# A four-layer graph kernel: the preparation ahead of its first stage reordered, part of it placed in that stage's first turn

## The reference

```python
# layer 0: two graph convolutions, then an LSTM over windows of length p = 1..4
h = relu(einsum('ts,bsh->bth', adj, x @ Wg0 + bg0))
h = relu(einsum('ts,bsh->bth', adj, h @ Wg1 + bg1))
for p in range(1, MAX_SKIP + 1):
    nw = Tv // p
    wins = h[:, :nw * p, :].reshape(Bv * nw, p, Hd)
    last = _lstm_last(Wih[p - 1], Whh[p - 1], bih[p - 1], bhh[p - 1], wins)
    h = h.at[:, arange(nw) * p + (p - 1), :].set(last.reshape(Bv, nw, Hd))
# layer 1: causal attention, scores + adj as mask; uses Wq Wk^T and Wv Wo
# layer 2: diagonal, upper and lower parts of adj with three weights W[k]
# layer 3: attention over 256 edges (src, dst), segments by src
e = einsum('behd,hd->beh', leaky_relu(Xq[:, src] + Xq[:, dst], 0.2), a)
e = e + log(adj[src, dst] + 1e-8)
attn = segment_softmax(e, src);  Y = segment_sum(attn * Xv[:, dst], src)
```

## Time and profile before

| | us |
|---|---|
| median of three runs | 1332.06 (1331.55 to 1334.45) |
| the profiled execution's own time | 1332.07 |
| its span, first to last instruction | 1330.3 |
| PE busy | 1208.8 (91%) |
| DVE busy | 1020.4 (77%) |
| ACT busy | 834.2 (63%) |
| POOL busy | 345.8 (26%) |
| mean granted TensorE clock | 0.977 of full speed |

### The profile page before, as it was taken

How to read it: one execution, slowest core, us unless ns; L and a number is a source line. 1 busy time by engine, 2 the same in 40 slices (tenths; PEclk the granted TensorE clock), 3 DMA queues, 4 the chain that set the end, 5 groups by cost and what they waited for, 6 DMA issues and landing times. The chain is left out here.

```text
span 1330.3 us, 25504 instructions
## 1 busy us (share of the span) xinstructions
PE 1208.8 (91%) x7808; PEld 1028.3 (77%) x7808; DVE 1020.4 (77%) x2892; ACT 834.2 (63%) x1836; POOL 345.8 (26%) x587
## 2 busy tenths in 40 slices
PE   2899999999899999999989799997999899978998
PEld 1678788787787877878878678876777688856998
DVE  6677877878778777787787699997777578776776
ACT  3476575675757757757567577775777376752332
POOL 3110200201002001020020122224667488842332
PEclk7899999999999999999999999998999899988999
DMA  9300000000000000000000000000000000001222
GB/s 272 84 1 1 1 1 1 0 0 0 0 0 0 0 0 0 0 0 0 0 1 1 1 1 0 0 0 1 1 0 0 0 2 1 2 1 32 75 75 71
DMA packets 24707, 20.85 MB, mean 16 GB/s; under 512 B 1744, under 2 KB 20304, under 8 KB 24400
## 3 DMA queue, kind: packets, MB, share of 16 engines
q1 hardware_dynamic: 24656, 20.21, 5.3%
HBM read 11.82 MB, written 8.39 MB: 15 GB/s over the span
## 5 line engine op out<-in xcount | busy, mean ns | idle before, releaser
L565 ACT ACTIVATE gate<-ps,b_lstm 128x256 f32<-128x256 f32 (+2 forms) x624 | 300.2, 557 | 36.8 <-PE ps L592 36.8
L590 PE MATMUL ps<-H_hi,w_hi 128*128 128x256 f32 (+2 forms) x624 | 212.7, 342 | 42.1 <-ACT gate L565 25.2
L591 PE MATMUL ps<-H_hi,w_lo 128*128 128x256 f32 (+2 forms) x624 | 205.4, 330 | 0.0
L592 PE MATMUL ps<-H_lo,w_hi 128*128 128x256 f32 (+2 forms) x624 | 196.1, 335 | 6.6 <-DVE H_lo L534 5.3
L575 ACT ACTIVATE tanh_c<-cell 128x512 f32<-128x512 f32 (+2 forms) x176 | 90.4, 514 | 127.7 <-DVE cell L525 81.7
L590 PEld LDWEIGHTS ps<-H_hi,w_hi 128*128 128x128 f32 x624 | 117.6, 189 | 68.1 <-ACT gate L565 32.6
L134 POOL TENSOR_SCALAR rstd<-mv 128x8 f32<-128x8 f32 x18 | 12.5, 694 | 601.0 <-DVE mv L107 600.9
L592 PEld LDWEIGHTS ps<-H_lo,w_hi 128*128 128x128 f32 x624 | 114.8, 189 | 25.1 <-DVE H_lo L534 17.4
L591 PEld LDWEIGHTS ps<-H_hi,w_lo 128*128 128x128 f32 x624 | 118.0, 189 | 7.7
L590 PE MATMUL ps<-hid_hi,w_hi 128*128 128x256 f32 (+2 forms) x384 | 119.2, 317 | 0.8 <-DVE hid_hi L531 0.8
L591 PE MATMUL ps<-hid_hi,w_lo 128*128 128x256 f32 (+2 forms) x384 | 117.4, 312 | 0.0
(11 more groups left out here) (203 smaller groups left out, 3034.4 us busy)
## 6 DMA issues: line engine op xcount, KB each, us to landing
out<-x SPq DMA_DIRECT2D x32, 256.0 KB, 2.3
w_raw<-in_WihT SPq DMA_DIRECT2D x1, 1024.0 KB, 8.4
w_raw<-in_WhhT SPq DMA_DIRECT2D x1, 1024.0 KB, 8.4
wqkvT<-in_WqkvT SPq DMA_DIRECT2D x1, 192.0 KB, 5.2
w_sb<-in_W SPq DMA_DIRECT2D x1, 192.0 KB, 4.9
ends_row<-in_src_row SPq DMA_DIRECT2D x1, 128.0 KB, 3.6
ends_row<-in_dst_row SPq DMA_DIRECT2D x1, 128.0 KB, 4.3
x<-in_x_in SPq DMA_DIRECT2D x8, 0.5 KB, 10.4
```

The source lines that it names most:

```text
L565: nc.scalar.activation(gate[:, g, z, 0:w * GB], gate_bank(g, k, m)[:, 0:w * GB], ACT.Tanh if z == G else ACT.Sigmoid, bias=b_lstm[:, 4 * ( ...
L590: nc.tensor.matmul(dst, w_hi[:, src, p - 1, z], v_hi, start=start, stop=False)
L591: return nc.tensor.matmul(dst, w_lo[:, src, p - 1, z], v_hi, start=False, stop=False)
L592: return nc.tensor.matmul(dst, w_hi[:, src, p - 1, z], v_lo, start=False, stop=stop)
```

## The change

What it does, part by part:

- The first 16 tiles of x are loaded in two halves (`ld_x0`, `ld_xb`), the first of them ahead of everything else on SP; behind it come the five loads that the graph convolutions need, the second half, three loads for layer 1, and the LSTM weights. The latter no longer have a buffer of their own: they land in the part of x that tiles 96 to 127 will take. The edge lists are three loads instead of four and are issued by ACT.
- The other 112 tiles of x and five late constants (`ld_late`) are issued by SP in the first stage's block. The load of tiles 96 to 111 waits until the weights have been split.
- On DVE the statistics of both halves stand ahead of the sort.
- The sort makes permutations already weighted with the edge ends (`moved`, fp32r) instead of a 0/1 permutation and replicated rows; TensorE multiplies them by ones: four fp32r matmuls for the rows, eight fp32 matmuls with one column for the column form (before: four fp32 matmuls and four with two columns).
- The split of the LSTM weights is made in seven pieces of 128x512 (one of the eight, for p = 1's hidden state, is never used) in items A0, OUT, W0 and U1 of group 0 of the first turn, high part on ACT, low part on POOL. TensorE waits for the pieces that a step uses (`w_low`).
- One-hot tables and edge marks are made on DVE in the first turn: seven operations in A0, the others in STEP+7 to STEP+10, where also the low part of layer 2's weights is made; POOL's six operations for layers 1 to 3 come at STEP+3. The logarithm is taken by ACT at the end of the first stage.

The diff, cut to its core:

```diff
@@ preparation, SP, ACT @@
-                for dst, s in ends:
-                    sp.dma_start(dst, s).then_inc(S["ld_e"], 16)
-                sp.dma_start(x[:, 0:NB, :], x_in[0:NB].rearrange("b t c -> t b c")).then_inc(S["ld_x0"], 16)
+                sp.dma_start(x[:, 0:GB, :], x_in[0:GB].rearrange("b t c -> t b c")).then_inc(S["ld_x0"], 16)
+                for dst, s in ((adjT_sb[:], adjT), (w_g[:, 0], Wg0), (w_g[:, 1], Wg1), (b0_col[:], bg0),
+                               (b1_bc[:], bg1.to_broadcast([P, P]))):
+                    sp.dma_start(dst, s).then_inc(S["ld_g"], 16)
+                sp.dma_start(x[:, GB:NB, :], x_in[GB:NB].rearrange("b t c -> t b c")).then_inc(S["ld_xb"], 16)
+                for dst, s in ((adj_sb[:], adj), (wqkvT[:], WqkvT.rearrange("(k d) c -> d k c", d=P)), (wo_sb[:], Wo)):
+                    sp.dma_start(dst, s).then_inc(S["ld_w"], 16)
+                for dst, s in ((raw_all[0], WihT), (raw_all[1], WhhT), (b_ih[:], bihT), (b_hh[:], bhhT)):
                     sp.dma_start(dst, s).then_inc(S["ld_lstm"], 16)
...
+                for dst, s in ((ends_row[:], src_row.to_broadcast([P, E])), (ends_col[:, 0], src_col),
+                               (ends_col[:, 1], dst_col)):
+                    act.dma_start(dst, s).then_inc(S["ld_e"], 16)
@@ preparation, DVE @@
+                for g in range(2):
+                    dve.wait_ge(S["ld_xb" if g else "ld_x0"], 16)
+                    norm_stats(g * GB, 0, GB, sa(g, "a_stats"), g * GB)
+                    wait_apart(dve, sa(g, "a_stats"), GB)
+                    norm_aggr(g * GB, GB, sa(g, "a_aggr"))
...
-                    link(nc.vector.tensor_scalar(perm[:, c], iota_e[:], rank[:, c:c + 1], None, ALU.is_equal))
                     for k in range(2):
-                        link(nc.vector.tensor_scalar(rep[:, k, c], ones[:], ends_colf[:, c, k:k + 1], None, ALU.mult))
+                        link(nc.vector.tensor_scalar(moved[:, k, c], iota_e[:], rank[:, c:c + 1],
+                                                     ends_colf[:, c, k:k + 1], ALU.is_equal, ALU.mult))
...
                 dve.wait_ge(S["pe_adj"], 1)
+                link(nc.vector.tensor_copy(picked[:].rearrange("p c m -> p (c m)"), ps[:, 4, 0:EC * P]))
@@ preparation, TensorE @@
-                        nc.tensor.matmul(ps[:, 0, k * E:(k + 1) * E], rep[:, k, c], perm[:, c],
+                        nc.tensor.matmul(ps[:, 0, k * E:(k + 1) * E], ones_r[:], moved[:, k, c],
                                          start=(c == 0), stop=(c == EC - 1))
...
+                            ins = nc.tensor.matmul(ps[:, 1, 2 * r + k:2 * r + k + 1],
+                                                   moved[:, k, c, r * P:(r + 1) * P].bitcast(F32), ones[:, 0:1],
+                                                   start=(c == 0), stop=(c == EC - 1))
@@ first stage @@
+        SPLITS = [(0, 0)] + [(src, p) for p in range(1, SKIPS) for src in range(2)]
+        SPLIT_AT = {A0: (0, 1), OUT: (1, 3), W0: (3, 5), U1: (5, 7)}
...
+                for i in range(1, TURNS):
+                    if i * NB == RAW:
+                        sp.wait_ge(S["w_low"], len(SPLITS))
+                    sp.dma_start(x[:, i * NB:(i + 1) * NB, :],
...
+                    if g == 0 and n in SPLIT_AT and opening(i):
+                        for k in range(*SPLIT_AT[n]):
+                            src, p = SPLITS[k]
+                            pool.wait_ge(S["w_high"], k + 1)
+                            nc.gpsimd.tensor_tensor(w_lo[:, src, p], raw_of(src, p),
+                                                    w_hi[:, src, p].bitcast(F32), ALU.subtract).then_inc(S["w_low"], 1)
...
+                    elif n == STEP + 9:
+                        link(nc.vector.tensor_tensor(picked[:], picked[:], hot_dT[:], ALU.mult))
+                        link(nc.vector.tensor_reduce(near[:], picked[:], AXX, ALU.add))
+                        nc.vector.tensor_scalar(near[:], near[:], LOG_EPS, None, ALU.add).then_inc(S["tab_made"], 1)
...
+                            nc.scalar.activation(w_hi[:, src, p], raw_of(src, p), ACT.Copy).then_inc(
+                                S["w_high"], 1)
...
+                act.wait_ge(S["tab_made"], 1)
+                nc.scalar.activation(log_a[:], near[:], ACT.Ln).then_inc(S["act_link"], 1)
...
+                    if opening(i):
+                        pe.wait_ge(S["w_low"], splits_of(p))
```

More of the change, by code:

```diff
@@ L549, in item @@
                                                  ACT.Copy).then_inc(sa(g, "a_ax"), 1)
-                    elif n == A1:
+                    if g == 0 and n in SPLIT_AT and opening(i):
+                        for k in range(*SPLIT_AT[n]):
+                            src, p = SPLITS[k]
+                            act.wait_ge(S["ld_lstm"], n_lstm)
+                            nc.scalar.activation(w_hi[:, src, p], raw_of(src, p), ACT.Copy).then_inc(
+                                S["w_high"], 1)
+                    if g == 0 and n == STEP and opening(i):
+                        act.wait_ge(S["b_made"], 1)
+                    if g == 0 and n == STEP + 9 and opening(i):
+                        act.wait_ge(S["ld_late"], n_late)
+                        nc.scalar.activation(w2_hi[:], w2_sb[:].rearrange("p k o -> p (k o)"), ACT.Copy).then_inc(
+                            S["w_high"], 1)
+                    if n == A1:
                         for c in range(CH):
```

220 lines of the change are left out of this document (110 added, 110 removed).

## The result

| | before | after |
|---|---|---|
| median of five runs each | 1333.16 (1331.55 to 1334.45) | 1326.55 (1324.67 to 1327.72) |
| ratio after / before, 95% interval | | 0.9946 (0.9933 to 0.996) |
| the profiled execution's own time | 1332.07 | 1327.72 |
| its span | 1330.3 | 1325.5 |
| first matmul of the first stage | 37.48 | 25.23 |

The kernel is faster by 6.6 us (0.5%). The sign and most of the mechanism were as forecast, the size was not: the gain forecast was 12, and the time lies 0.55 above the upper end of the range. The kernel before now has a median 1.1 above the 1332.06 that the forecast started from; that start times the ratio gives 1324.9, inside the range. A second series of five on another chip gave 1326.06 and a ratio of 0.9942 (0.9928 to 0.9955).

What follows compares the result with a forecast made beforehand. The preparation was taken to be added to the end, bound by two chains ending together: the sort with the weight splits, and the issue of seven 1 MB loads. 1332.1 - 14.7 + 2.7 = 1320.1, forecast 1320, range 1315 to 1326.

Steps and rivals of the forecast that it cites:

- signs that it named as wrong: Stage's start after 26; U1 load wait over 2 us; DVE operations 1.3 or more beside POOL; issue-idle in first 30.
- step 1: Preparation: the second half of x, issued at 3.4, lands 5.6 later, at 9.0; bounds 7.6 and 10.2.
- step 3: Preparation: the sort on DVE takes 4.0 instead of 4.6, ending at 15.3.
- step 4: Preparation: first sort matmul to DVE's copy takes 3.6 instead of 4.9, with 1.0 for the four fp32r matmuls.
- steps 2 and 5: Preparation, DVE: second half's statistics and aggregations 2.3; after the sort, copies, `hot_s` and adjacency matmuls 2.9.
- step 6: End of the preparation's block: 1.0 until the stage's first matmul, at 22.8.
- STEP+7 to +10: First turn: the operations put there, 4.0 us on DVE, cost 2.7; bounds 0 and 4.5.
- (a): Stage starts at the full clock, A0's 32 records take 4.1 instead of 6.3: 1318; chance 0.24.
- (b): Preparation: halves of x take 10.5 instead of 5.6 to land, moving DVE's chain by 4.9: 1325; chance 0.10.
- (c): First turn: POOL's seven subtractions hold DVE, 8.9 us in front of operations TensorE waits for: 1329; chance 0.04.
- (d): First turn: loads of x slow instruction fetches, up to 10.5 each on TensorE's chain; with two, 1341; chance 0.06.
- (e): First turn: the moved table operations find room: 1317.4; chance 0.56 together with the forecast.

Runs made afterwards that it cites:

- splits back: Kernel after, with the seven weight split pieces made in the preparation again, on the same engines: 1329.24, ratio 0.9972 to the kernel before.
- old sort: Kernel after, with the sort's 0/1 permutation and replicated rows of the kernel before: 1326.95, ratio 0.9954 to the kernel before.
- busy: Kernel after, with seven more fp32 matmuls, their result unused, on TensorE ahead of the sort: 1324.97, ratio 0.9946 to the kernel before.
- the last kernel: Kernel after with bias wait in A1, second statistics behind sort, three tables in A0, adjacency diagonal in preparation, four unused fp32 matmuls: 1319.31, ratio 0.9899 to before.

## Why the prediction was right in sign and wrong in size

The reading of what bounds the kernel held: the preparation is added to the end, and two chains end it. The loads and the splits, each put back alone, do hold up the new order, by 5.6 and 3.8 us. Every cover that the prediction named for moved work held too, where the work was looked at: POOL's subtractions and ACT's pieces ("splits back"), the load of tiles 16 to 31 and the last logarithm cost nothing. None of the signs that it named as wrong came. Short of the forecast are these terms, from the rows of the profile after:

| term | forecast | measured | lost |
|---|---|---|---|
| step 1, second half of x landed | 9.0 | 10.6 | 1.6 |
| step 3, sort on DVE | 4.0 | 4.2 | 0.2 |
| step 4, sort's matmuls to DVE's copy | 3.6 | 4.5 | 0.9 |
| steps 2 and 5 | 5.2 | 5.35 | 0.1 |
| step 6, end of the block | 1.0 | 0.55 | -0.4 |
| first turn, opening up to H_hi | 0 | 0.36 | 0.4 |
| first turn, ACT's table load | not seen | 1.35 | 1.35 |
| first turn, STEP+7 to +10 | 2.7 | 3.3 | 0.6 |

The sum is 4.7, and 12.0 - 4.7 = 7.3 against the 7.66 found at the second stage's start; the turns' 0.4 make up the difference. The medians show 6.6 and, in the second series, 7.5.

- Step 1 failed in the issue more than in the landing. The load was issued at 4.77, not 3.4, mostly because the two `w_g` issues held SP for 1.84 where 0.43 each was taken from other small loads; the landing itself took 5.8 for the 5.6 forecast. The start of the statistics was outside the bound given for it (10.2). Why the two issues took longer is not shown; ACT issued its three loads at the same time, from 0.81 to 2.36.
- Step 4: the four fp32r matmuls took the 1.0 taken for them. The column form was scaled from matmuls in two-column form at 0.17 a record; it took 0.21. The 0.17 was a mean of two rates: in the trace of before, those eight records begin 0.21 apart up to 15.29 and 0.12 apart at the end, so the clock rose among them. The forecast took the lower clock for the row form and this mean for the column form.
- The table load was the one cost with no term at all. The rivals asked what the added waits would hold, but not what a second wait on the first gate would do to the table load ahead of it.
- Step for STEP+7 to +10: 3.3 within the bounds 0 to 4.5. The choice near the upper part was right and still short; DVE's waits for gates gave back 0.7 of 4.0, not 1.3.
- The 0.36 of the opening is no cost of the moved work: 0.30 of it is the length of A0 (6.59 instead of 6.29).
- One sum was off without effect: seven pieces of 1.27 from 42.5 end at 51.4, not 51.9.

Of the rivals, (a) the full clock in A0 did not come (6.59); with the old sort it did (3.81), which points to the light matmuls that the text held against it, but rests on one execution. (b), the late landing, did not come: the half took 5.8 to land, not 10.5; step 1 was late by a third of (b)'s 4.9 for the other reason above. (c), the held DVE, did not come, but the lock exists: two runs met it. (d), stalls from fetched instructions, did not come: in the stage's first 30 us, at a DMA share of 0.94 (window below), the instruction queues moved one packet, as many as in the same stretch before, and the first turn's loss is accounted for by its three parts.

```profile
25.20:55.20 30.00, 27.06 (x143) 22.15 (x144) 20.25 (x55) 17.28 (x30) 11.80 (x11) 1.00 0.94 260
```

(e), room for the table operations, did not come where they were put; it came in A0.

What stays open: what decides the drop of the clock at the second stage's opening and how often either kernel meets it, why it falls in the first two turns of some kernels, and what the old sort is worth over many executions.

## What to carry to other kernels

When several chains end together, moving all but one out gives only the distance to the one that is left: order that one next, and fill its waits (the statistics in the sort's wait gave 2.4 us of start). Moved work is free by its place, not by its size: the same DVE operations cost 3.3 us where DVE goes from group to group without a pause and nearly nothing beside matmuls that DVE waits for, if no GpSimd work holds the port there. After adding a wait to an activation that changes the function table, look in the trace where the table load went.

## What the runs showed of the hardware

- A table load takes over one of two waits of the activation behind it: 2.40 us of idle time ahead of it and 1.28 exposed; with one wait less it ran 3.7 sooner and beside the matmuls. Nine profiles with both waits and five with one agree.
- fp32 matmul records with one moving column take 0.21 us at the lower clock (3.41 for 16) and 0.12 at the upper one (1.84 for 16 in the last kernel), the same as records with 128 columns: A0's 32 take 6.59, 0.21 each, and with the old sort 3.81, 0.12 each.
- The clock can fall while TensorE reads as busy: at 18.9 after 2 us of such records, with a pause of 1.02 us ahead of them ("busy"). The printed clock is also to be read with care ahead of its first change: in the window below, of the kernel after, it reads 1.00, but six records in the microsecond are the lower rate; with the old sort the same window holds eleven.

```profile
26.00:27.00 1.00, 1.00 (x6) 1.00 (x6) 0.89 (x4) 0.00 (x0) 0.00 (x0) 1.00 0.25 50
```

```profile
26.00:27.00 1.00, 1.00 (x11) 1.00 (x11) 0.89 (x4) 0.60 (x1) 0.00 (x0) 1.00 0.29 67
```

- A 1 MB load of x held SP for 3.2 us with others ahead of it still moving (mean of 5 in 16.04), the first of them for 0.86; a 1 MB load of LSTM weights, in rows of 8 KB where those of x are of 512 bytes, for 0.43 (at 7.05 in after); small loads for 0.43, and now and then twice that.
- Two operations of DVE that need two SBUF inputs took 1.67 each instead of 0.69 beside POOL's subtractions, and POOL's seven took 9.52 instead of 8.66.
